# State-space and convolution kernel: the inputs of states 0 and 2 of an item in one GpSimd product, and two buffers for u

## What is computed

```python
dt = softplus(dbc[..., :DT_RANK] @ W_dt.T + b_dt)
def step(h, inp):
    dt_t, B_t, C_t, x_t = inp
    dA = exp(dt_t[:, :, None] * A)
    h = dA * h + (dt_t * x_t)[:, :, None] * B_t[:, None, :]
    return (h, einsum('bdn,bn->bd', h, C_t))
y = ys + xc * D_skip
y = y * silu(z)
```

## Time and profile before

| | |
|---|---|
| median of three runs | 812.57 us |
| profiled execution, its own time | 813.16 us |
| its span in the profile | 811.4 us |
| TensorE, busy share of the span | 91% (736.3 us) |
| VectorE | 90% (727.4 us) |
| ScalarE | 89% (724.0 us) |
| GpSimd | 85% (690.6 us) |
| granted TensorE clock, mean | 0.994 of full |

### The profile page before, as it was taken

The page is one execution under the profiler, slowest core; times in us unless marked ns, Lnnn a source line. Parts: engine busy times, 40 slices in busy tenths (PEclk is TensorE's granted clock), DMA queues, the critical chain, the costliest instruction groups (busy, mean ns, idle before and its releaser), DMA issues.

```text
span 811.4 us, 13741 instructions
## 1 busy us (share of the span) xinstructions
PE 736.3 (91%) x4854; PEld 398.2 (49%) x4854; DVE 727.4 (90%) x488; ACT 724.0 (89%) x1358; POOL 690.6 (85%) x211
## 2 busy tenths in 40 slices
PE   8798989898989999898989898989899897899998
PEld 4544444444454444444444444444535444557876
DVE  4799999999999999999999999999999999995141
ACT  5899999999999999999999999999999999865050
POOL 0579999999999999999999999999999999980000
PEclk9899999999999999999999999999999999999999
DMA  7807061626253443625161616253533525100011
GB/s 208 302 18 270 17 249 53 232 96 218 84 189 114 157 147 108 220 66 211 45 232 56 238 62 225 105 200 102 180 122 124 180 66 188 37 2 1 0 40 65
DMA packets 40173, 106.05 MB, mean 131 GB/s; under 512 B 8012, under 2 KB 11176, under 8 KB 40104
## 3 DMA queue, kind: packets, MB, share of 16 engines
q1 hardware_dynamic: 38476, 104.87, 37.7%
q10 hardware_dynamic: 1628, 0.30, 0.2%
HBM read 102.01 MB, written 3.15 MB: 130 GB/s over the span
## 4 chain that ended last, share of the span: by engine, by line
PE 37%; ACT 28%; DVE 15%; issue 10%; POOL 8%; DMA 1%; ACTq 1%; POOLq 0%; DVEq 0%
DVE state L1030 12%; PE bank L1261 11%; ACT product L772 9%; PE bank L1547 8%; PE bank L1254 6%; ACT state L752 6%; ACT bank L741 5%; POOL state L648 4%; POOL state L659 4%; PE bank L1240 3%; DVE bank L1030 2%; PE bank L1287 2%; ACT dt L802 2%; PE bank L1315 2%; ACT xc L787 1%
## 5 line engine op out<-in xcount | busy, mean ns | idle before, releaser
L659 POOL TENSOR_TENSOR state<-state,wide 128x2048 f32<-128x2048 f32 (+1 forms) x104 | 407.9, 3954 | 6.2 <-DVE state L1030 6.2
L648 POOL TENSOR_TENSOR state<-u,wide 128x1024 f32<-128x1024 f32 (+1 forms) x77 | 248.9, 3252 | 25.4 <-DVE state L997 24.3
L1261 PE MATMUL bank<-state,ident 64*64 64x512 f32 x2048 | 252.6, 604 | 11.5 <-POOL state L659 11.3
L1030 DVE TENSOR_TENSOR_SCAN state<-bank,state 128x1024 f32<-128x1024 f32 x109 | 246.8, 2276 | 5.3 <-POOL state L648 3.0
L772 ACT ACTIVATE product<-u_tok,b_tok 128x256 f32<-128x256 f32 x588 | 247.8, 498 | 3.0 <-PE bank L1254 2.9
L1254 PEld LDWEIGHTS bank<-ident,product 128*128 128x128 f32 x1176 | 128.8, 140 | 136.2 <-issue 107.8
L1254 PE MATMUL bank<-ident,product 128*128 128x128 f32 x1176 | 156.1, 276 | 40.9 <-DVE state L1030 29.4
L752 ACT ACTIVATE state<-dt,a_neg 128x512 f32<-128x512 f32 x294 | 192.9, 710 | 0.0
L1030 DVE TENSOR_TENSOR_SCAN bank<-state,bank 128x1024 f32<-128x1024 f32 x77 | 173.9, 2276 | 1.2 <-PE bank L1254 1.2
L1030 DVE TENSOR_TENSOR_SCAN state<-state,bank 128x1024 f32<-128x1024 f32 x70 | 158.4, 2268 | 3.6 <-PE bank L1254 3.2
L741 ACT ACTIVATE bank<-dt,a_neg 128x512 f32<-128x512 f32 x218 | 140.7, 676 | 3.6 <-DVE state L1030 3.1
(11 more groups left out here) (103 smaller groups left out, 471.5 us busy)
## 6 DMA issues: line engine op xcount, KB each, us to landing
wide<-bc_rows SPq DMA_DIRECT2D x159, 512.0 KB, 5.6
wide<-bc_rows SPq DMA_DIRECT2D x47, 256.0 KB, 3.8
x_t<-in_x_dram SPq DMA_DIRECT2D x4, 512.0 KB, 5.9
out_dram<-x_t SPq DMA_DIRECT2D x8, 256.0 KB, 2.0
k_room<-in_L_conv_w_dram SPq DMA_DIRECT2D x2, 576.0 KB, 6.4
bc_rows<-dbc SPq DMA_DIRECT2D x32, 32.0 KB, 1.5
state<-in_L_conv_W_in_dram SPq DMA_DIRECT2D x2, 256.0 KB, 3.9
x_tok<-in_x_dram ACTq DMA_DIRECT2D x1, 256.0 KB, 3.7
```

What stands on the lines that cost most here:

```text
L648: pool.tensor_tensor(tiles(group), u_for(len(group)), rows(b_wide, PLAIN.index(s), len(group)), ALU.mult).then_inc(plain_input, 1)
L659: pool.tensor_tensor(tiles(group), tiles(group), rows(c_wide, group[0] % NST, len(group)), ALU.mult).then_inc(output_pool, 1)
L1030: dve.tensor_tensor_scan(flat(target), flat(decay), flat(source), 0.0, ALU.mult, ALU.add).then_inc(scanned, 1)
L1261: return pe.matmul(y_sum[64 * h:64 * h + 64, b, :], weights[rows, :], source[rows, h, :], start=first, stop=last)
```

## The change

`times_b` of states 0 and 2 of the next item becomes one instruction of 128x2048 elements, at the place where state 0 had its own; the one of state 2, at the end of the item, goes. The two slots of its output lie two apart (or, when the ring wraps, slots 8 and 0). Item 0 keeps them apart. Its row loads stay two (`B_LOADS`), and the product waits for both. u gets a second buffer, so that `make_u(k)` waits for the inputs and transposes of item k - 2 and no longer for those of item k - 1. Nothing else moves. The diff, cut to its core:

```diff
-B_GROUPS = ((0,), (2,), (4, 5), (10, 11), (13,),)
+B_GROUPS = ((0, 2), (4, 5), (10, 11), (13,))
+B_LOADS = ((0,), (2,), (4, 5), (10, 11), (13,))
...
 def b_group(n):
+    if n < NST and n % NST in B_GROUPS[0]:
+        return (n,)
     group = next(q for q in B_GROUPS if n % NST in q)
...
-        u = sb("u", [128, HALVES, CHUNK])
+        u = [sb(f"u{m}", [128, HALVES, CHUNK]) for m in range(2)]
...
-            return state[:, a:b + 1, :, :] if b == a + 1 else state[:, a::b - a, :, :]
+            return state[:, a:b + 1:b - a, :, :] if b > a else state[:, a::b - a, :, :]
...
 def times_b(n):
-                wait(pool, b_loaded[next(q for q in range(len(B_GROUPS)) if s in B_GROUPS[q])], 16 * (k + 1))
+                for q, states in enumerate(B_LOADS):
+                    if any(m % NST in states for m in group):
+                        wait(pool, b_loaded[q], 16 * (k + 1))
                 for m in group:
                     wait_slot_free(pool, m)
-                pool.tensor_tensor(tiles(group), u_for(len(group)), rows(...), ALU.mult)
+                pool.tensor_tensor(tiles(group), u_for(k, len(group)), rows(...), ALU.mult)
...
 def make_u(k):
-                wait(pool, u_tok_mm, 2 * k)
-                wait(pool, plain_input, plain_inputs(NST * k))
-                pool.tensor_tensor(u[:, :, :], dt[m][:, :, :], xc[m][:, :, :], ALU.mult)
+                wait(pool, u_tok_mm, 2 * (k - 1))
+                wait(pool, plain_input, plain_inputs(NST * (k - 1)))
+                pool.tensor_tensor(u[m][:, :, :], dt[m][:, :, :], xc[m][:, :, :], ALU.mult)
...
                 times_b(n + 16)
                 times_c(n + 13)
-                times_b(n + 18)
```

More of the change, by code:

```diff
@@ L286, in mamba_conv_kernel @@
         rows_stored = sem("rows_stored")
-        b_loaded = [sem(f"b_loaded{q}") for q in range(len(B_GROUPS))]
+        b_loaded = [sem(f"b_loaded{q}") for q in range(len(B_LOADS))]
         c_loaded = [sem(f"c_loaded{q}") for q in range(len(C_GROUPS))]
@@ L373, in rows, with u_for @@
             return wide_rows[:, first:first + count, :].unsqueeze(2).to_broadcast([128, count, HALVES, CHUNK])
-        def u_for(count):
+        def u_for(k, count):
             if count == 1:
-                return u[:, :, :]
-            return u[:, :, :].unsqueeze(1).to_broadcast([128, count, HALVES, CHUNK])
+                return u[k % 2][:, :, :]
+            return u[k % 2][:, :, :].unsqueeze(1).to_broadcast([128, count, HALVES, CHUNK])
         def flat(halves):
@@ L555, in store_rows @@
                 if k >= 2:
-                    for q in range(len(B_GROUPS)):
+                    for q in range(len(B_LOADS)):
                         sp.wait_ge(b_loaded[q], 16 * (k - 1))
@@ L572, in spread_b @@
             def spread_b(k, q):
-                states = B_GROUPS[q]
+                states = B_LOADS[q]
                 if all(is_turned(NST * k + s) for s in states):
@@ L637, in times_b @@
                     return
-                group = [m for m in (n - n % NST + s for s in next(q for q in B_GROUPS if n % NST in q)) if not is_turned(m)]
-                if not group:
+                if is_turned(n):
                     return
+                group = b_group(n)
                 k, s = n // NST, group[0] % NST
@@ L644, in times_b @@
                     pool.wait_ge(plain_input, 1)
-                wait(pool, b_loaded[next(q for q in range(len(B_GROUPS)) if s in B_GROUPS[q])], 16 * (k + 1))
+                for q, states in enumerate(B_LOADS):
+                    if any(m % NST in states for m in group):
+                        wait(pool, b_loaded[q], 16 * (k + 1))
                 for m in group:
                     wait_slot_free(pool, m)
-                pool.tensor_tensor(tiles(group), u_for(len(group)), rows(b_wide, PLAIN.index(s), len(group)),
+                pool.tensor_tensor(tiles(group), u_for(k, len(group)), rows(b_wide, PLAIN.index(s), len(group)),
                                    ALU.mult).then_inc(plain_input, 1)
@@ L666, in make_u @@
                 wait(pool, xc_ready, 2 * k + 2)
-                wait(pool, u_tok_mm, 2 * k)
-                wait(pool, plain_input, plain_inputs(NST * k))
-                pool.tensor_tensor(u[:, :, :], dt[m][:, :, :], xc[m][:, :, :], ALU.mult).then_inc(u_ready, 1)
+                wait(pool, u_tok_mm, 2 * (k - 1))
+                wait(pool, plain_input, plain_inputs(NST * (k - 1)))
+                pool.tensor_tensor(u[m][:, :, :], dt[m][:, :, :], xc[m][:, :, :], ALU.mult).then_inc(u_ready, 1)
             def pads():
@@ L984, in first_u @@
                 dve.wait_ge(dt_ready, HALVES)
-                dve.tensor_tensor(u[:, :, :], dt[0][:, :, :], xc[0][:, :, :], ALU.mult).then_inc(u_ready, 1)
+                dve.tensor_tensor(u[0][:, :, :], dt[0][:, :, :], xc[0][:, :, :], ALU.mult).then_inc(u_ready, 1)
             def cut_sequences(k):
@@ L996, in first_input @@
                 dve.wait_ge(u_ready, 1)
-                dve.tensor_tensor(tile(0), u[:, :, :], over_halves(b_wide[:, 0, :]), ALU.mult).then_inc(plain_input, 1)
+                dve.tensor_tensor(tile(0), u[0][:, :, :], over_halves(b_wide[:, 0, :]), ALU.mult).then_inc(plain_input, 1)
             def magnitudes(n):
@@ L1342, in turn_u @@
                         mm = pe.transpose(u_tok_place(k, j)[:, E_IN * i + 128 * h:E_IN * i + 128 * h + 128],
-                                          u[:, h, 128 * (2 * j + i):128 * (2 * j + i) + 128], ident[:, :])
+                                          u[k % 2][:, h, 128 * (2 * j + i):128 * (2 * j + i) + 128], ident[:, :])
                 mm.then_inc(u_tok_mm, 1)
```

## The result

The changed kernel took 808.05 us, median of five runs (807.41 to 809.27), against 812.57 of before (811.35 to 813.13): a ratio of 0.995, 95% interval 0.9939 to 0.9962. A second series of six gave 808.78 against 812.35, 0.996 (0.9948 to 0.9973). So it is 3.6 to 4.5 us faster.

The account below looks back on a forecast made before the run. GpSimd was taken as the bound, 43.37 us an item. 13 x 0.35 = 4.55 us saved, less the later input of state 0, left 2.39, with state 2's wait gone 2.61: from 812.57 to 810.0 us, range 808.5 to 812.8.

Parts of the forecast that it names:

- GpSimd sets the pace: Steady items: GpSimd's own sum, 43.31 us, makes the item of 43.37; VectorE at 42.93 and ScalarE at 42.92 are close behind.
- a wait of VectorE before the scan of state 0: Sign in VectorE's timeline: it waits there alone, right behind the merged product, touching already at item 3.
- 0.14 for one instruction less: GpSimd, states 0 and 2: two single products cost 4.64 us, a pair 4.50, so 0.14 us saved an item.
- No charge for slots that lie apart: Merged product's output: the distance between its two slots adds nothing; bounds 0.02 us cheaper and 0.06 dearer.
- rival of a dearer product: Merged product on GpSimd costs x more than another pair; with x = 0.35 us the time is 814.9 us; chance 0.12.
- rival of the merge alone: Wait at `make_u` worth nothing: 1.82 us saved, 2.17 paid, 0.22 back, 0.1 us faster, 812.5 us; chance 0.19.
- 0.21 for the wait of GpSimd on its own product: In front of `make_u`: the second buffer of u removes this wait, 0.21 us an item; bounds nothing and 0.21.
- GpSimd's item falls to 43.02: Steady items: GpSimd's item falls by 0.35 us from 43.37 to 43.02, still the slowest by 0.09.
- The later input costs 2.17 once and not per item: Scan of state 0 waits for the longer product; GpSimd runs 2.17 us further ahead, with 2.47 of room at state 10.
- 0.22 at state 2: VectorE's second wait for GpSimd, before the scan of state 2, goes: 0.22 us.
- The rest of the last item shifts as a whole: Last item: VectorE and TensorE set the end and shift as a whole; nothing more is gained there.
- the pair of 108.25 us: Start of GpSimd's path, last held by a scan; 13 items from there save 4.55 us, scan 0 comes 2.39 earlier.

Follow-up runs that it names:

- two_u: Kernel before with only the second buffer of u, states 0 and 2 keeping a product each: 809.4 us, 0.9962 of before.
- merge_wait: Changed kernel with the merged product but the old waits in front of u: 812.62 us, 1.0006 of before.
- split_1011: Changed kernel with the product of states 10 and 11 cut into two, one GpSimd instruction more an item: 811.97 us, 0.9994 of before.
- short_c13: Changed kernel with the C product of state 13 cut to 16 of 512 columns in items 0 to 14: 808.3 us, 0.995 of before.
- after_again: The changed kernel once more, unedited, for a second profile: 808.78 us, 0.996 of before.
- late_pair: Changed kernel with the merged product one place later, behind the C product of state 13: 846.1 us, 1.0422 of before.
- before_pad: Kernel before with a second buffer beside u that nothing uses: 811.89 us, 0.9995 of before.
- before_start: Kernel before, unedited, one execution to look at its start: 812.46 us.
- before_warm: Kernel before with transposes of ident that nobody reads put into TensorE's waits in items 0 and 1: 811.76 us, 0.9994 of before.
- warm pair: before_warm and the changed kernel with the same unread transposes in TensorE's waits: 811.76 and 808.31 us.

## Why the prediction was right, and where it was short

- **GpSimd sets the pace, before and after.** Right. two_u and merge_wait, which touch GpSimd's work alone, move the items by what they take from GpSimd, and split_1011 moves them back. Of the signs that the text had given, one did not show as written: a wait of VectorE before the scan of state 0. It is there, 0.06 us from item 2 on, but too short to be printed. Items of 42.9 us without any wait would have meant that another engine sets the pace; 42.98 is close to that, and it takes split_1011 and short_c13 to tell the two apart.
- **0.14 for one instruction less.** 0.17 by merge_wait, 0.15 by split_1011. No charge for slots that lie apart: right, 4.51 us. The rival of a dearer product is out. In the rival of the merge alone the text has a sign wrong: 1.82 saved and 0.22 back against 2.17 paid make it 0.1 us slower, 812.7, not 0.1 faster. merge_wait's 812.62, with an interval of about 0.9 us to either side, cannot tell the two.
- **0.21 for the wait of GpSimd on its own product.** 0.24 by two_u. The Trainium skill, "VectorE: DVE Perf Modes", section "The DRAIN you can't avoid", which says that a semaphore between two instructions of VectorE is free, must not be carried over to GpSimd: the runs here show 0.24 us for it. That GpSimd's completion holds up what waits for its semaphore but not the next instruction stands in the Trainium skill, "GPSIMD Engine Reference", section "Instruction dispatch"; the trace agrees, with 2.54 us from start to start with the wait and 2.31 without.
- **GpSimd's item falls to 43.02.** 42.98. Here the sum was 0.04 short. Between the anchors of the two profiles, GpSimd's 13 items took (681.11 - 108.25) - (674.56 - 106.73) = 5.03 us less, 0.387 an item instead of 0.35, which is 0.48 more than the 4.55 of the sum. With 0.04 off for the last product's duration (4.59 instead of 4.55) it is the 0.44 us by which the gain behind that anchor (2.83) exceeded the forecast (2.39). The two terms themselves came as forecast: averaged from start to start over items 8 to 12, the wait gave 0.21 (2.54 to 2.32) and the merge 0.14 (4.65 to 4.50). The other 0.04 an item lie scattered over products that the change does not touch; in after_again it is only 0.01, and why is open.
- **The later input costs 2.17 once and not per item.** Right, and the point on which it all hung. Scan 0 starts 0.03 behind the product, from item 2 on (item 3 had been forecast); the pair (9, 10) stands 0.13 behind the scan of state 10 (0.2 forecast). late_pair shows the other side of the limit.
- **0.22 at state 2.** 4.60 (688.16 to 683.56) against 4.35 at state 0: 0.25.
- **The rest of the last item shifts as a whole.** Right: from the scan of state 2 to the last gate 39.30 before, 39.28 after.
- **Not in the sum: the start.** 1.5 us of the 4.7 between the two profiled spans are the place of the low clock. Item 0 differs by 1.4 us between two executions of the changed kernel (42.79 and 44.21), and by 1.2 between two of the old one (43.04 and 44.21). The forecast took the steps of items 0 and 1 in one execution as fixed. Within the first profiles this luck helped the change; it is no part of its gain.
- **Not in the sum: what counts as the start of GpSimd's path.** The text anchored it at the pair of 108.25 us, in front of which GpSimd waited 0.34 us for a scan. In before_pad, before_start and before_warm, where TensorE's clock did not fall in item 1, that wait is not there: GpSimd is full from the pair (9, 10) of item 0 on, and item 1 is a GpSimd item too. In before_start its two pairs start at 63.87 and 107.60, 43.73 us apart (u of item 2 waits 0.52 there); in the changed kernel, after_again, they start at 63.74 and 106.77, 43.03 apart. That is 0.70 us more to gain, and it shows in the rests, which are 0.5 to 0.8 longer in these three profiles than in the first. 2.6 as forecast and 0.5 for the item make 3.1; 3.18 were measured in the pair with the low clock in item 1. With 0.7 for item 1 it is 3.8; 3.77 were measured in the pair without. Only the warm pair, 3.2 or 3.4 without its last low stretch, falls short of 3.8, and that is open. So the forecast's mechanism was right and its 2.6 us too small by 0.5 to 1.2, by the two terms above; its wide range, not its sum, held the second median.

What each part is worth. The second buffer carries nearly all: by the rests without a low clock in item 1 it gives 3.5 us alone (699.65 to 696.13), by the medians 2.95. The merge adds 0.25 us to it (696.13 to 695.88), and alone 0.3 (698.89 to the 698.6 of merge_wait); the medians say 0.6 more and 0.3 less, with intervals of about 1 us to either side, so that more than "little" is not shown for it. The reason is in the sum: the merge lowers GpSimd's sum by 2.1 us over the items and pays about as much once for the later input.

## What to carry to other kernels

When an engine is the bound by a few tenths of a microsecond an item, add up its own starts first, and then write down every loop that leads through another engine: a product that comes later is paid once as long as its engine can run ahead, and per item from the point where a loop closes (one place in the order was worth 37 us here). A wait of an engine on its own semaphore is a cost of its own; a second buffer that removes it can be worth more than an instruction less. And cut the start off before two profiles are compared, and then compare those whose starts were alike: a shift that is already there at the first steady item is not the change's until a second profile says so.

## What was not expected of the hardware

The granted clock of TensorE fell to the lower level in item 0 of every profile of an execution of usual length. Without the added transposes it fell during or up to about 2 us behind a wait of TensorE of 1.4 us, anywhere between about 21 and 26 us. In item 1, where TensorE waits 1.2 us in all of these profiles, it fell in before, after, merge_wait and split_1011 only; in short_c13 it fell in item 2 instead. An item 1 with it took 44.12 us on VectorE, without it 42.9. Transposes put into those waits kept the clock at 1.00 there, and it fell at about 31 us instead, where TensorE waits next (1.5 and 1.8 us); the times moved by 0.06%, inside the interval. What decides in which executions it falls, and when, no run here shows.
